# Gate phases on GpSimd and VectorE, and a clearing moved out of the set-up

## What is computed

```python
xn = _layernorm(x)
out = segment_sum(xw[src] * alpha, dst) .reshape(N, 256) + gnn_bias   # alpha = ex / denom[dst]
x = x + relu(out) + mix(xn)
y = _layernorm(x)                                   # the rows that the experts take
topk_vals, topk_idx = top_k(y @ gate_w + gate_b, 2) # 16 experts, two are chosen
x = x + ffn(y)                                      # each chosen expert's two matmuls, weighed and normalised
```

## Time and profile before

| | us |
|---|---|
| median of 3 runs | 3071.61 |
| lowest and highest run | 3068.89, 3074.11 |
| profiled execution, its own time | 3075.73 |
| its span in the profile | 3074.0 |
| TensorE, VectorE, ScalarE, GpSimd busy | 2528.0, 2112.2, 1434.7, 1977.0 |

### The profile page before, as it was taken

How to read it: one execution, slowest core, us unless ns; L and a number is a source line. 1 busy time by engine, 2 the same in 40 slices (tenths; PEclk the granted TensorE clock), 3 DMA queues, 4 the chain that set the end, 5 groups by cost and what they waited for, 6 DMA issues and landing times. The chain is left out here.

```text
span 3074.0 us, 52974 instructions
## 1 busy us (share of the span) xinstructions
PE 2528.0 (82%) x12108; PEld 1639.8 (53%) x12108; DVE 2112.2 (69%) x5060; ACT 1434.7 (47%) x3421; POOL 1977.0 (64%) x2089
## 2 busy tenths in 40 slices
PE   5999888889788978887888888797864528999996
PEld 2555445445445455544545454444443527888884
DVE  8888877777777777767777777777777834333335
ACT  3444465556555555555555646454532311222227
POOL 4666767777777777777777777777773571222224
PEclk9999999999998999999998989999986559999998
DMA  6222244554545454545455455444442165777777
GB/s 170 44 46 44 63 140 137 151 143 136 150 137 143 137 150 137 143 144 142 137 150 143 138 143 143 143 136 143 137 136 85 67 209 174 232 233 232 233 239 254
DMA packets 297444, 450.53 MB, mean 147 GB/s; under 512 B 116374, under 2 KB 193467, under 8 KB 297190
## 3 DMA queue, kind: packets, MB, share of 16 engines
q0 software_dynamic: 86320, 241.77, 27.8%
q1 hardware_dynamic: 183142, 134.74, 15.8%
q10 hardware_dynamic: 27744, 71.38, 7.0%
HBM read 393.49 MB, written 55.83 MB: 146 GB/s over the span
## 5 line engine op out<-in xcount | busy, mean ns | idle before, releaser
L216 POOL DMA_INDIRECT rows_g<-node_rows,idx x1564 | 1489.5, 952 | 483.4 <-issue 446.9
L1196 PE MATMUL p_m<-msg,sel 128*128 128x264 f32 x3512 | 986.2, 429 | 236.5 <-DVE msg L1164 191.8
L1196 PEld LDWEIGHTS p_m<-msg,sel 128*128 128x128 f32 x3512 | 688.3, 206 | 363.2 <-issue 252.5
L1164 DVE TENSOR_TENSOR msg<-rows_g,p_w 128x1024 f32<-128x1024 f32 x439 | 534.7, 1218 | 42.9 <-ACT p_w L1062 41.2
L1062 ACT ACTIVATE p_w<-lg 128x32 f32<-128x32 f32 x439 | 88.3, 201 | 721.7 <-DVE lg L1157 716.2
L1867 POOL DMA_INDIRECT moe<-ysb,token x120 | 116.3, 969 | 349.2 <-DVE ysb L1854 324.2
L1017 ACT ACTIVATE sel_t<-apart,ones 128x512 bf16<-128x512 bf16 x442 | 319.0, 722 | 31.2 <-issue 1.1
L1153 DVE TENSOR_TENSOR lg<-rows_g,ends 128x32 f32<-128x32 f32 x439 | 86.3, 196 | 352.7 <-SPq L996 249.4
L1086 DVE TENSOR_TENSOR sel<-p_w,dst_t 128x512 f32<-128x512 f32 x440 | 303.1, 689 | 21.8 <-issue 5.3
L1014 ACT ACTIVATE apart<-dst_all,iota_neg 128x512 bf16<-128x512 bf16 x442 | 312.5, 707 | 0.0
L1040 ACT ACTIVATE qfeat<-p_scr 128x512 f32<-128x512 f32 x442 | 239.5, 588 | 103.3 <-PE p_scr L1219 98.8
(11 more groups left out here) (340 smaller groups left out, 3323.0 us busy)
## 6 DMA issues: line engine op xcount, KB each, us to landing
dst_all<-dst_bc ACTq DMA_DIRECT2D x112, 512.0 KB, 4.2
wa<-in_L_ffn_w_dram SPq DMA_DIRECT2D x64, 512.0 KB, 4.8
wb<-in_L_ffn_w_dram SPq DMA_DIRECT2D x64, 512.0 KB, 5.3
rows_g<-node_rows,idx POOLq DMA_INDIRECT x1564
xs<-slot_x SPq DMA_DIRECT2D x56, 258.0 KB, 2.9
ya<-moe SPq DMA_DIRECT2D x48, 256.0 KB, 4.6
bb<-in_L_ffn_b_dram SPq DMA_DIRECT2D x64, 128.0 KB, 5.5
qs<-xn_turned ACTq DMA_DIRECT2D x13, 512.0 KB, 5.5
```

What stands on the lines that cost most here:

```text
L216: pool.indirect_dma_start(rows_g[:, j, u, :], None, node_rows, bass.IndirectOffsetOnAxis(ap=idx[q][:, j, u:u + 1], axis=0)).then_inc(gathe ...
L1164: dve.tensor_tensor(m4, g3[:, :, 0:D].rearrange("p u (h e) -> p u h e", h=H), p_w[:, 0:TC * H].rearrange("p (u h) -> p u h", u=TC).unsquee ...
L1196: mm = pe.matmul(p_m[j % 2][:, 0:ROW], sel[j][:, u, :], msg[j % 2][:, u, :], start=(u == 0), stop=(u == TC - 1))
```

## The change

In the gate: VectorE inverts the denominators of the first 16 tiles in one go and signals it (`inverses_ready`). GpSimd, which has a wait for that signal in front of its indirect DMAs now, scales and adds the bias for phases 1 and 2, which are tiles 4 to 9 and 10 to 15, in four instructions over 128x1536 elements. VectorE's part of these phases is the new function `add_to_rows`, the second half of `residual`, and waits for GpSimd's semaphore `pool_made`. `norm(1)` stands ahead of `choose(0)` now. The phases have 4, 6, 6, 10, 12 and 12 tiles instead of 4, 6, 10, 10, 10 and 10. In the set-up: the clearing of `acc` leaves GpSimd's list and stands at the start of GpSimd's list in the block of keys and values; the six writes of zeros go from SP's queue to GpSimd's, where the clearing stood, behind a wait for `zrow`.

```diff
@@ -345,8 +345,6 @@
                 lo = LIST_TILES * LIST_CHUNKS
                 tail = src[lo * CHUNK:full * CHUNK].rearrange("(a b) -> a b", b=CHUNK)
                 sp.dma_start(src_lists[:, lo:full, :], tail.rearrange("a (p u) -> p a u", u=u4)).then_inc(tail_out, 16)
-                for t in range(T, TQ):
-                    sp.dma_start(xn_turned[t * P:(t + 1) * P, :], zrow[:]).then_inc(scratch_out, 16)
                 sp.wait_ge(copied, len(turns) + 1)
                 sp.dma_start(b1_cols.rearrange("e p c -> p e c"), b1_t[:].rearrange("p (e c) -> p e c", e=NEXP)).then_inc(scratch_out, 16)
                 for g in range(G4):
@@ -355,7 +353,7 @@
                 sp.wait_ge(lists_padded, 16)
                 sp.dma_start(src_lists[0:last, full:full + 1, :].rearrange("p a u -> p (a u)"),
                              src[full * CHUNK:E].rearrange("(p u) -> p u", u=u4)).then_inc(tail_out, 16)
-                sp.wait_ge(scratch_out, (TQ - T + G4 + 1) * 16)
+                sp.wait_ge(scratch_out, (G4 + 1) * 16)
 
             @block.gpsimd
             def _(pool):
@@ -378,7 +376,9 @@
                     p0 = (h % HALF) * C
                     pool.dma_start(t_col[p0:p0 + C, h // HALF:h // HALF + 1], heads[h:h + 1].unsqueeze(0).broadcast_to([C, 1])).then_inc(b_in, 16)
                 pool.dma_start(bq_col[:], bqkv[0:D].rearrange("(g p) -> p g", p=P), allow_slow_non_contiguous=True).then_inc(b_in, 16)
-                pool.memset(acc_flat[:, 2 * H * FEAT:T * ROW], 0.0)
+                pool.wait_ge(pads_set, 3)
+                for t in range(T, TQ):
+                    pool.dma_start(xn_turned[t * P:(t + 1) * P, :], zrow[:]).then_inc(b_in, 16)
                 pool.wait_ge(dst_padded, 5 * 16)
                 pool.wait_ge(b_ready, 1)
                 for g in range(G4):
@@ -469,7 +469,7 @@
                 dve.reciprocal(rstd[:], rstd[:])
                 dve.drain()
                 dve.scalar_tensor_tensor(out=nmr[:], in0=mv[:, :, 0], scalar=-1.0, in1=rstd[:], op0=ALU.mult, op1=ALU.mult)
-                dve.wait_ge(b_in, (3 + H + 1) * 16)
+                dve.wait_ge(b_in, (3 + H + 1 + TQ - T) * 16)
                 dve.tensor_scalar(t_col[:], t_col[:], SCALE * SCALE, None, ALU.mult)
                 dve.wait_ge(meet_turned, 1)
                 dve.tensor_copy(meet[:, 0:FCH, :], p_meet[:, 0:FCH * C].rearrange("p (m i) -> p m i", i=C))
@@ -837,6 +837,7 @@
                     pool.tensor_tensor(tail[:, :, 0, :, :], k4[:, :, :, 0:C], k4[:, :, :, DIAGS - 1:WRAP], ALU.mult)
                     pool.tensor_copy(tail[:, :, 1, :, :], k4[:, :, :, 0:C]).then_inc(pool_feats, 1)
 
+                pool.memset(acc_flat[:, 2 * H * FEAT:T * ROW], 0.0)
                 pairs(pool, T, body)
                 for s in range(2):
                     pool.wait_ge(row_out[s], T // 2 * 16)
@@ -1299,8 +1300,8 @@
 
 
         late = ExitStack()
-        SPANS = ((0, 4), (4, 10), (10, 20), (20, 30), (30, 40), (40, T))
-        PHASES, TP = len(SPANS), 10
+        SPANS = ((0, 4), (4, 10), (10, 16), (16, 26), (26, 38), (38, T))
+        PHASES, TP = len(SPANS), 12
         xl = acc[:, :, 0:D]
         top_w = sb("top_w", [P, T, 2], ctx=late)
         places = sb("places", [P, 2, T], I32, ctx=late)
@@ -1330,7 +1331,8 @@
             oh_pos = [sb(f"oh_pos{i}", [P, TP, NEXP], ctx=c) for i in range(2)]
             own_i = sb("own_i", [P, T], I32, ctx=c)
             spread_e = sb("spread_e", [P, P], ctx=c)
-            own_set = sem("own_set", c)
+            pool_made = sem("pool_made", c)
+            inverses_ready = sem("inverses_ready", c)
             cnt = sb("cnt", [P, TP, NEXP], ctx=c)
             tri = sb("tri", [P, P], ctx=c)
             pos = sb("pos", [P, TP, NEXP], ctx=c)
@@ -1416,6 +1418,10 @@
                         a = acc[:, lo:hi, 0:D]
                         dve.tensor_tensor(a, a, b_gnn[:].unsqueeze(1).broadcast_to([P, hi - lo, D]), ALU.add)
                     dve.drain()
+                    add_to_rows(ph)
+
+                def add_to_rows(ph):
+
                     for lo, hi in PARTS[ph]:
                         r, a = resid[:, lo:hi, :], acc[:, lo:hi, 0:D]
                         dve.scalar_tensor_tensor(out=r, in0=a, scalar=0.0, in1=r, op0=ALU.max, op1=ALU.add)
@@ -1442,14 +1448,19 @@
                     dve.reciprocal(w, w)
                     dve.drain()
 
-                invert(*SPANS[0])
+                early = SPANS[2][1]
+                w = acc[:, 0:early, D:ROW]
+                dve.tensor_scalar(w, w, TINY, None, ALU.max)
+                dve.drain()
+                dve.reciprocal(w, w).then_inc(inverses_ready, 1)
+                dve.drain()
                 residual(0)
-                invert(SPANS[0][1], T)
-                dve.wait_ge(own_set, 1)
+                invert(early, T)
+                dve.wait_ge(pool_made, 1)
                 norm(0)
                 dve.memset(zpad[:, :, 0:D], 0.0)
                 dve.memset(zpad[:, :, D + 1:XROW], -1.0)
-                dve.wait_ge(own_set, 1)
+                dve.wait_ge(pool_made, 1)
                 dve.tensor_copy(zpad[:, :, D:D + 1], zpad_i[:].unsqueeze(2)).then_inc(zpad_set, 1)
                 dve.memset(keep[:], 1.0)
                 dve.memset(toe[:], 0.0)
@@ -1525,7 +1536,17 @@
                     dve.tensor_copy(places[:, :, span], placef[:, :, span]).then_inc(places_ready, 1)
 
 
-                for ph in range(1, PHASES):
+                dve.wait_ge(pool_made, 2)
+                add_to_rows(1)
+                norm(1)
+                choose(0)
+                place(0)
+                dve.wait_ge(pool_made, 3)
+                add_to_rows(2)
+                choose(1)
+                norm(2)
+                place(1)
+                for ph in range(3, PHASES):
                     residual(ph)
                     choose(ph - 1)
                     norm(ph)
@@ -1666,7 +1687,15 @@
                 pool.affine_select(out=tri[:], in_=ones[:], compare_op=ALU.is_ge, fill=0.0, base=-1,
                                    pattern=[[1, P]], channel_multiplier=-1).then_inc(tri_ready, 1)
                 pool.iota(zpad_i[:], [[1, SLOT_ROWS // P]], base=2 * NP, channel_multiplier=SLOT_ROWS // P)
-                pool.iota(own_i[:], [[2 * P, T]], base=0, channel_multiplier=2).then_inc(own_set, 1)
+                pool.iota(own_i[:], [[2 * P, T]], base=0, channel_multiplier=2).then_inc(pool_made, 1)
+                pool.wait_ge(inverses_ready, 1)
+                for ph in (1, 2):
+                    lo, hi = SPANS[ph]
+                    a = acc[:, lo:hi, 0:D]
+                    a4 = a.rearrange("p t (h e) -> p t h e", h=H)
+                    pool.tensor_tensor(a4, a4, acc[:, lo:hi, D:ROW].unsqueeze(3).broadcast_to([P, hi - lo, H, C]), ALU.mult)
+                    pool.drain()
+                    pool.tensor_tensor(a, a, b_gnn[:].unsqueeze(1).broadcast_to([P, hi - lo, D]), ALU.add).then_inc(pool_made, 1)
                 for ph, (lo, hi) in enumerate(SPANS):
                     pool.wait_ge(places_ready, ph + 1)
                     for t in range(lo, min(hi, BLOCKS)):
```

## The result

The changed kernel takes 3078.70 us in the median of 13 runs (3074.91 to 3084.31), the kernel before 3071.61 (3067.89 to 3074.63, 13 runs): ratio 1.0025, 95% interval 1.0017 to 1.0032, or 7.1 us. The profiled execution has a span of 3080.7 us against 3074.0; TensorE is busy 2522.1 us, VectorE 2112.0, ScalarE 1434.8 and GpSimd 1994.4, 17.4 more than before.

What follows compares the result with a forecast made beforehand. The gate was taken to end at GpSimd's last wait for VectorE plus the remaining indirect DMAs. -4.6 (gate) + 12.0 (waits) - 0.4 (set-up) = +7.0 us on 3071.6, forecast 3078.6; range for 8 in 10: 3066 to 3083.

Steps and rivals of the forecast that it cites:

- VectorE waits behind all four instructions of GpSimd: Gate, phase 0: the two engines alternate, delaying VectorE 12.0 us; the forecast case, chance 0.60, 3075.5 to 3081 us.
- The upper bound: Gate, phase 0: VectorE waits for each of GpSimd's four whole instructions; the other bound was no wait at all.
- The size, 12.0 us: Gate, phase 0: VectorE's moments start at 2376.1 instead of 2364.05, with 3.45 us for each GpSimd instruction.
- my lower bound of 2.85: Lowest estimate, in us, for one GpSimd instruction of 1536 elements; 3.45 was taken, 3.8 the highest.
- -4.6 us without waits: Gate: with no engine in another's way, the last indirect DMA ends at 2529.8 instead of 2534.4.
- P3: Gate: the moment VectorE's `places` of phase 3 are ready, 2443.3 without waits; 66 DMAs stand behind it.
- Only TENSOR_SCALARs wait: Rival, chance 0.17: only this kind falls behind GpSimd's instructions, about 7.1 us late, +2.5 in the gate, 3073.7 us.
- nothing waits: Rival, chance 0.18: VectorE never waits behind GpSimd in the gate, so -4.6 - 0.4, 3066.6 us.
- The set-up, -0.4 with +0.7 at worst: Set-up: L422 may end earlier, but `x` binds and the zeros may delay it; -0.4 us, range -1.5 to +0.7.
- The first half: Set-up: L422 ends at about 13 if GpSimd's six issues of zeros hold it, otherwise 5.4 us earlier.
- The second half: Set-up: the last piece of `x` lands at 36.2, so no more than 1.5 us can be gained.
- The clearing's new place: Start of next block: L742 waits up to 1.7 us for the clearing, hidden by 2.31 us idle before L760.

Runs made afterwards that it cites:

- with PSUM: Changed kernel with one PSUM operand in each large VectorE instruction of phase 0, bn_aggr moments, second inversion behind the constants: 3079.65 us, 1.0008 to the kernel before.
- later start: Changed kernel with GpSimd signalled only after VectorE's third large instruction of phase 0: 3078.03 us, ratio 1.0024 to the kernel before.
- one phase helped: Changed kernel's gate, all VectorE operands in SBUF, GpSimd helping phase 1 only, old phases and old set-up: 3079.62 us, ratio 1.0016 to the kernel before.
- with PSUM and one phase: PSUM operands in phase 0, GpSimd helping phase 1 only, old phases, clearing moved, zeros in SP's queue: 3067.04 us, 0.9986 to before; again 3073.60, 0.9992.
- without the help: Changed kernel without GpSimd's four instructions, VectorE doing all; new phases, order and set-up kept: 3080.55 us, ratio 1.0013 to the kernel before.
- The clearing alone: Kernel before with only GpSimd's clearing memset moved to just before its first pair, zeros staying in SP's queue: 3071.91 us, ratio 1.0000.

## Why the prediction came out right, step by step

- **VectorE waits behind all four instructions of GpSimd**: right, with the order of turns as written down, L1411, L1419, L1427 and a moment. The upper bound was the right end. The first DMA started at 2392.49 (2394.6 had been said), the last wait of GpSimd ended at 2453.81 (2455), and the last DMA at 2540.52 (2542). The ledger holds in five kernels to 0.1 us: from the first DMA without help, add what VectorE's held instructions lost and take off 3.66 for the scale and bias of phase 1 (1.83 us of VectorE for each). Changed kernel 30.4 + 9.67 - 3.66 = 36.4, measured 36.3; with PSUM 30.4 + 4.59 - 3.66 = 31.3, measured 31.2; later start 30.4 + 10.13 - 3.66 = 36.9, measured 36.8; one phase helped 30.3 + 5.67 - 3.66 = 32.3, measured 32.2; with PSUM and one phase 30.3 - 3.66 = 26.6, measured 26.5.
- **The size, 12.0 us**: too large by 2.3. I had 3.45 us for each of GpSimd's instructions. The additions of the bias take 3.43 alone, so the line through the earlier trace rows held for them; the multiplications take 2.77, under my lower bound of 2.85. In turns GpSimd's four take 2.77, 3.27, 2.63 and 3.28, in all 11.95 and not 13.8, which is 1.85 of the 2.3; VectorE's take 1.08 to 1.09 each from turn to turn and not 1.23, which is 0.44.
- **-4.6 us without waits**: 184.4 less the 9.7 of waits is 174.7, 3.8 less than before; 0.8 too good. Of this I had not seen that it is a loss and a gain: the new phases cost 4.3 to 4.5, and four instructions less in each of two phases give 8.4 back (183.1 without the help, 174.7 with it and without its waits). P3 in the changed kernel is at 97.7 us; by my sum with the measured delay it is 2443.3 - 2355.9 + 9.7 = 97.1. Behind it I had 86.5 us for the DMAs, and they took 86.7.
- **"Only TENSOR_SCALARs wait" and "nothing waits"**: both fell. L117, a TENSOR_TENSOR on 128x4 numbers, waits as the large ones do.
- **The set-up, -0.4 with +0.7 at worst**: the one step that failed. The next block starts 1.25 us later in the profile, not earlier. The first half was open, and the answer is that GpSimd's DMA issues do not hold L422. The second half, that `x` lands when it did before, was wrong: it came later, and VectorE, now early, waited for it. The clearing alone shows 1.5 us early once and the time unchanged. Of the 1.25 us, 0.32 are left at L760 (53.52 against 53.20), and kernels with the old set-up differ there by 1.1 among themselves (52.12 to 53.20). In the whole time this term cannot be told from zero (0.9998).
- **The clearing's new place**: L742 waited 1.35 us, the idle time before L760 took it in, as said.
- **The sum**: +7.0 forecast, 7.1 measured. In the profile it is +5.8 in the gate where +7.4 stood, and +0.3 at its start. SP fetches 5.0 us later (2544.75 against the earlier trace rows), and the span is 6.7 longer, so 1.6 us lie in the experts, where nothing was changed. From SP's fetch to the end the profiles of all these kernels take 531.7 to 536.6 us with the same instructions (534.3 before, 536.0 changed), so the 1.6 are within what this stage scatters, and nothing has to explain them. The gate was thus forecast 1.6 us too high, and what filled the sum up again cannot be told from scatter. That 7.0 and 7.1 lie so near is luck; the measured 7.1 itself has an interval of 5 to 10 us. The mechanism is not luck: it is in the ledger.

## What to carry to other kernels

Work given to an idle GpSimd is free only while VectorE runs instructions that GpSimd cannot hold; beside others, each of GpSimd's instructions costs VectorE up to its full length, here 5.7 us for two of them against a saving of 3.7, whether VectorE's own instruction has 1024 elements or four. Before moving such work, write down everything that VectorE issues until GpSimd is through, the constants too; one operand in PSUM takes a large instruction out of the conflict, and a shorter piece of help can be worth more than a longer one. When the phases of a pipeline are resized in the same edit, time them by themselves: here they cost 4.3 of the 5.8 us by which the gate grew, and the help, its saving taken off, 1.3.

## What the runs showed of the hardware

- The exclusion of VectorE and GpSimd goes in turns, and the profile shows no idle time for it: it lengthens the instruction that waits. GpSimd's multiplication took 2.77 us undisturbed and 3.75 behind VectorE, its addition 3.43 and 4.20.
- It holds for TENSOR_TENSOR, SCALAR_TENSOR_TENSOR, TENSOR_SCALAR and CAST down to 128x2 numbers (1.71 us instead of 0.16). It does not hold for BATCH_NORM_STATS2 (1.41 either way), for a RECIPROCAL (0.19 at 2366.35, with GpSimd busy from 2366.20), nor where one of two operands is in PSUM (1.22).
- GpSimd's memset, which only writes, holds a TENSOR_SCALAR (L742, 1.53 us instead of 0.18), while the direct DMAs that GpSimd issues beside L422 do not hold it (0.35 us, the issues run from 2.43 to 12.65).
